# Score order by array half, and first-pass products of two heads issued in turn, in a macaron attention kernel

## What is computed

```python
        q = (qkv @ Wq + bq).reshape(B, S, H, dh).transpose(0, 2, 1, 3)
        k = (qkv @ Wk + bk).reshape(B, S, KVH, dh).transpose(0, 2, 1, 3)
        ...
        scores = jnp.einsum('bhgqd,bhkd->bhgqk', qg, k) * scale
        ...
        bias = slopes.reshape(KVH, G, 1, 1) * rel
        causal = jnp.tril(jnp.ones((S, S), dtype=bool))
        bias = jnp.where(causal, bias, -jnp.inf)
        attn = jax.nn.softmax(scores + bias[None], axis=-1)
        out = jnp.einsum('bhgqk,bhkd->bhgqd', attn, v)
```

## Time and profile before

| | |
|---|---|
| median of 3 runs | 739.92 us (739.89 to 741.77) |
| profiled execution, its own time | 740.43 us |
| its span on the core | 738.6 us |
| TensorE busy | 702.6 us (95%) |
| VectorE busy | 582.3 us (79%) |
| ScalarE busy | 403.3 us (55%) |
| reductions at L903, VectorE | 352 of them, 223.0 us, 681 ns each |
| L896, VectorE: reductions that also add the causal mask | 256 records, 149.3 us |
| attention, in the trace | from about 190 to about 600 us |

### The profile page before, as it was taken

How to read it: one execution, slowest core, us unless ns; L and a number is a source line. 1 busy time by engine, 2 the same in 40 slices (tenths; PEclk the granted TensorE clock), 3 DMA queues, 4 the chain that set the end, 5 groups by cost and what they waited for, 6 DMA issues and landing times.

```text
span 738.6 us, 15927 instructions
## 1 busy us (share of the span) xinstructions
PE 702.6 (95%) x5906; PEld 365.6 (50%) x5906; DVE 582.3 (79%) x1921; ACT 403.3 (55%) x579; POOL 112.6 (15%) x122
## 2 busy tenths in 40 slices
PE   8999998967999999999999999999999889999998
PEld 4554487833344444444444444444444255554598
DVE  6976468697999999999999999999999238766311
ACT  3353332132667777776777777677777743353300
POOL 3202882110000000000000000000000002103950
PEclk9999999975899999999999999999999999999999
DMA  8014533442010011001100100110010000005531
GB/s 217 1 16 77 93 64 113 144 139 85 25 38 26 27 26 40 20 21 38 33 26 20 39 20 22 39 38 20 21 39 1 2 1 0 2 1 91 107 92 58
DMA packets 47249, 34.69 MB, mean 47 GB/s; under 512 B 13106, under 2 KB 46514, under 8 KB 47172
## 3 DMA queue, kind: packets, MB, share of 16 engines
q1 hardware_dynamic: 46596, 33.60, 18.6%
q10 hardware_dynamic: 576, 0.08, 0.1%
HBM read 23.01 MB, written 10.39 MB: 45 GB/s over the span
## 4 chain that ended last, share of the span: by engine, by line
PE 52%; DVE 13%; issue 11%; ACT 2%; DVEq 0%; ACTq 0%
PE ps L1018 49%; DVE mx L903 8%; PE ps L1023 4%; DVE mx L896 1%; ACT h_all L624 1%; DVE h_all L896 1%; DVE xn L705 1%; DVE stats L693 0%; DVE wb L923 0%; DVE mm_ L920 0%; DVE sg L838 0%; ACT osb L613 0%; DVE idle L894 0%; DVEq L133 0%; DVE mv L697 0%
## 5 line engine op out<-in xcount | busy, mean ns | idle before, releaser
L624 ACT ACTIVATE h_all<-ps 128x1024 f32<-128x1024 f32 (+3 forms) x384 | 291.3, 810 | 112.4 <-PE ps L1018 109.2
L903 DVE TENSOR_REDUCE mx<-ps 128x1 f32<-128x512 f32 (+2 forms) x352 | 223.0, 681 | 9.2 <-PE ps L1018 5.8
L1018 PE MATMUL ps<-ks,xnT_all 57*128 57x512 bf16 (+3 forms) x768 | 178.9, 337 | 15.6 <-DVE mx L896 6.4
L1018 PE MATMUL ps<-h_all,vb 128*32 128x512 f32 (+3 forms) x1536 | 163.8, 500 | 0.6 <-ACT osb L613 0.6
L1018 PE MATMUL ps<-xnT_all,ks 59*128 59x512 bf16 (+3 forms) x768 | 158.6, 331 | 3.6 <-ACT h_all L624 3.4
L896 DVE CUSTOM_DVE_ANT_0 h_all<-ps,mask_w 128x384 bf16<-128x384 f32 (+1 forms) x256 | 149.3, 618 | 2.3 <-issue 0.7
L1018 PEld LDWEIGHTS ps<-ks,xnT_all 57*128 57x128 bf16 x768 | 56.5, 94 | 143.4 <-DVE mx L896 64.9
L1018 PE MATMUL ps<-cb 64*128 64x64 bf16 (+3 forms) x1216 | 113.0, 215 | 0.0
L717 DVE TENSOR_TENSOR h_all<-ps,sg 128x512 f32<-128x512 f32 x80 | 55.2, 690 | 50.5 <-PE ps L1018 48.8
L563 ACT ACTIVATE sg<-ps 128x512 f32<-128x512 f32 x80 | 47.8, 597 | 82.6 <-PE ps L1018 82.3
L1018 PEld LDWEIGHTS ps<-cb 64*128 64x128 bf16 x1216 | 80.1, 96 | 17.3 <-issue 0.7
(11 more groups left out here) (120 smaller groups left out, 553.6 us busy)
## 6 DMA issues: line engine op xcount, KB each, us to landing
xnT_all<-q_scr SPq DMA_DIRECT2D x64, 96.0 KB
attn<-sel_scr SPq DMA_DIRECT2D x12, 256.0 KB, 7.2
mask_second<-sel_scr SPq DMA_DIRECT2D x12, 256.0 KB, 8.2
q_scr<-qp SPq DMA_DIRECT2D x8, 384.0 KB
ks<-k_scr SPq DMA_DIRECT2D x64, 48.0 KB
x<-in_x SPq DMA_DIRECT2D x8, 256.0 KB, 5.7
yT<-sel_scr SPq DMA_DIRECT2D x8, 256.0 KB, 9.0
q_scr<-qp SPq DMA_DIRECT2D x8, 256.0 KB
```

The costliest lines, as they stand in the source:

```text
L624: act.activation(pr[:, (NSTEP * i + s) % PR_BUFS, p:HPG:SLOTS, lo:HALF], ps[:, b:b + 2, lo:HALF], ACT.Exp)\
L903: dve.tensor_reduce(m, src, AX.X, V.max).then_inc(a_out, 1)
L1018: return pe.matmul(o, l, r, start=start, stop=stop, skip_group_check=True)
```

## The change

Three things are changed.

- `score` issues the product of the half that the last piece did not use first, and its mask products in that order too. `RowsUsed.last` keeps the half of the last piece (0 upper, 1 lower) while the order is written out. Before, it was upper, then lower.
- Two merged pieces of the same shape that stand in the same group are issued by `two_pieces`: both banks are asked for first, then the products are issued one from each in turn, and each of the two last products raises `a_in`. This meets pieces 0 and 1 (step 0), 10 and 11 (step 3), 16 and 17 (step 5) of units 1 to 15, and 0 and 1 of unit 0.
- In `PER_STEP`, step 5 goes from (0, 2, 0, 1) to (0, 1, 0, 2): piece 16 moves from ahead of the step's second score pair to behind the product with V, where piece 17 already stood.

```diff
-PER_STEP = [(2, 1, 0, 0), (0, 1, 1, 0), (0, 2, 2, 1), (0, 2, 0, 0), (0, 3, 0, 0), (0, 2, 0, 1),
+PER_STEP = [(2, 1, 0, 0), (0, 1, 1, 0), (0, 2, 2, 1), (0, 2, 0, 0), (0, 3, 0, 0), (0, 1, 0, 2),
...
+            class RowsUsed:
+                last = 1
+
+            def piece_products(i, n, b):
...
+                RowsUsed.last = h0 // SLOTS
...
+            def two_pieces(i, n):
+
+                upper, lower = slot(a_out, NP1 * i + n + 1), slot(a_out, NP1 * i + n + 2)
+                for first, second in zip(piece_products(i, n, upper), piece_products(i, n + 1, lower)):
+                    pass
+                first.then_inc(a_in, 1)
+                second.then_inc(a_in, 1)
+                RowsUsed.last = PIECES[n + 1][1] // SLOTS
+
+            def pieces_of(i, some):
+
+                n = some.start
+                while n < some.stop:
+                    together = n + 1 < some.stop and PIECES[n][2] > 1 and PIECES[n][2:] == PIECES[n + 1][2:]
+                    if together:
+                        two_pieces(i, n)
+                    else:
+                        piece(i, n)
+                    n += 2 if together else 1
...
-                for r in range(2):
+                order = (1 - RowsUsed.last, RowsUsed.last)
+                for r in order:
                     at = RG * r
...
-                        for r in range(2):
+                        for r in order:
```

## The result

| | before | after |
|---|---|---|
| median, 6 runs each | 739.9 us (737.95 to 741.77) | 744.23 us (743.71 to 745.41) |
| ratio, 95% interval | | 1.0058 [1.0041, 1.0075] |
| span of the profiled execution | 738.6 us | 741.9 us |

The forecast was 743.0 us, in a range of 739.0 to 745.2, slower likeliest. It is slower, by 4.3 us where 3.1 were forecast. So the sign and most of the size were right, and 1.2 us are missing from the sum.

A forecast was written before the change was run, and what follows sets the result against it. The prediction took a TensorE chain that enters VectorE once per 25.70 us unit, at piece 17's reduction, as the bound. Terms 0 + 0 + 0 + 0.20 us over 15 units add 3.1 to 739.92: 743.0 us, range 739.0 to 745.2.

The forecast's parts named there:

- The bound: TensorE's chain per 25.70 us unit enters VectorE once, at piece 17's 0.70 us reduction (432.57); making it later lengthens the unit.
- Part 1: Turned score pairs, 12 of 24 a unit: lower product already overtakes the upper, so 0; at best 0.05 us.
- The first rival: Score products start in program order, so turned pairs in step 8 save up to 0.44 us a unit: 736.3 us; chance 0.16.
- Part 2: Pieces 0 and 1 issued in turn: they already run side by side, so 0.
- Part 3: Pieces 10 and 11 in turn: piece 10's reduction 0.25 us later, TensorE loses nothing; 0, at most 0.1 us a unit.
- the margin of 0.01 us at piece 14: Piece 11's reduction now ends at 428.71; with 0.05 for release, piece 14's start near 428.76 is met by 0.01 us.
- Part 4: Pieces 16 and 17 behind the product with V: TensorE 0.41 us ahead, piece 17's reduction late, 0.20 us a unit lost.
- Nothing is given back behind 434: From 434 to 440.7 the chain is TensorE's own work, so everything keeps its spacing and the 0.20 us delay stays.
- the rival "no change": VectorE's waits elsewhere, such as 0.28 us before 438.70, take up the delay: about 740 us; chance 0.17.
- The sum: All four parts, 0 + 0 + 0 + 0.20 us a unit over 15 units: 3.1 us slower, 743.0 us.

The follow-up runs named there:

- move_only: Kernel before with only step 5 of PER_STEP at (0, 1, 0, 2), piece 16 behind the product with V: 743.32 us, ratio 1.0043, unit +0.19 us.
- between: Kernel before with step 5 at (0, 1, 1, 1), piece 16 between the second score pair and the product with V: 738.15 us, ratio 0.9974, unit -0.10 us.
- flip_only: Kernel before with only the turned score pairs, the half not used last going first: 739.59 us, ratio 0.9994, unit 25.70 us.
- flip_wrong: Kernel before with each score pair starting with the half that was used last: 739.92 us, ratio 0.9996, unit 25.71 us.
- merge_load_apart: Kernel before with pieces 0/1 and 10/11 in turn, covered first-bank wait left out, load wait moved from piece 10 to 7: 740.88 us, ratio 1.0005, unit +0.09.
- merge_only: Kernel before with only pieces 0 and 1, and 10 and 11, issued in turn: 741.91 us, ratio 1.0023, unit +0.16 us.
- changed_load_apart: Whole changed kernel with the covered first-bank wait left out and the load wait moved from piece 10 to piece 7: 743.73 us, ratio 1.0054, unit +0.20.

## Why the prediction was right, and where it was not

- **The bound.** Right. The reduction at 432.57 sets the unit: in move_only, between and the changed kernel the unit moved by what that reduction moved, to 0.02 us, and the same operation in VectorE's slack cost nothing.
- **Part 1, score pairs, 0.** Right in both directions, flip_only and flip_wrong. The changed kernel's own step 8 looks like the earlier trace rows:

```profile
440.57 0.39 PE L1018 MATMUL ps<-ks,xnT_all 57*128 57x512 bf16 x1
440.58 0.33 PE L1018 MATMUL ps<-xnT_all,ks 59*128 59x384 bf16 x1
...
440.80 0.32 PE L1018 MATMUL ps<-xnT_all,ks 59*128 59x384 bf16 x1
```

  The first rival, faster by program order of the starts, falls with these and with the pair of step 5 above. It also speaks against the rule of the Trainium skill that the prediction weighed (TensorE: Matmul & The Clock Gate, The mechanism), that matmuls start strictly in program order: by it flip_wrong would have cost what flip_only gained, and neither did anything.
- **Part 2, pieces 0 and 1, 0.** Right as far as it can be seen: merge_load_apart's loss is accounted for by pieces 10 and 11. It wasn't run alone.
- **Part 3, pieces 10 and 11, 0 with a bound of 0.1.** The step that failed is the sentence that TensorE loses nothing because both pieces now do what piece 11 did. They do it 0.09 us later. I had the row of the double wait in hand (`[waits a_out,a_ld_second_even]` ahead of piece 10) and took the start of piece 11, which has a single wait, as its price. Everything behind followed: piece 10's reduction 0.34 late and not 0.25, piece 12's 0.17 and not 0.08. The stated bound of 0.1 a unit, 1.5 us, covered it by luck, since it was set for another reason, the margin of 0.01 us at piece 14. That margin did not decide: piece 14 starts 0.22 behind piece 12 before and after. The bank that VectorE's lateness reaches in merge_only is piece 16's, two pieces later, which I hadn't followed. With the late start taken away, the rest of part 3 holds in the changed kernel: changed_load_apart has piece 12 0.09 late and yet a unit of +0.20, the move alone.
- **Part 4, the move, 0.20 a unit.** Right, step by step. Product with V 0.53 behind piece 15; pieces 16 and 17 directly behind it and side by side; piece 17's reduction 0.61 behind piece 16's; piece 21 0.05 behind piece 18's end. Piece 16's reduction stands 0.83 behind piece 15's (434.27 - 433.44), not 0.9, because piece 15's was 0.16 late and TensorE, which delivers piece 16, only 0.10. move_only has it without that: 0.90, and a unit of +0.19.
- **Nothing is given back behind 434.** Right. From piece 18's reduction to VectorE's next wait the spacing is 5.39 us before and after (435.61 to 441.00):

```profile
441.00 2.73 DVE L903 TENSOR_REDUCE mx<-ps 128x1 f32<-128x512 f32 x4 [0.28 <-PE ps L1018]
```

  The wait of 0.28 is the same as in the earlier trace rows, so the rival "no change" falls too.
- **The sum.** Forecast 15 x 0.20 = 3.1 us, measured 4.3 in the medians and 4.2 by the unit. The mis-sized term is part 3's, put at 0: without its late start the unit falls from 25.98 to 25.91, unrounded by 0.08, and 15 x 0.08 = 1.2 us is what lies between 743.0 and 744.23.

## What to carry to other kernels

Before interleaving the two halves of the array by hand, look whether their products already start side by side; if so, the order pays nothing, and what counts is when the last product behind a semaphore is delivered to the engine that the chain of waits enters, and which instruction waits for that bank one turn of the ring later. A piece moved behind a longer product gives TensorE a lead that it can only spend waiting, if the reductions are the link: move it just so far that the reducing engine's queue has no gap (here 0.10 us a unit, and 0.20 lost by going one product further). When a wait is moved to an earlier instruction, see which waits that instruction already has.

## What the runs showed of the hardware that I had not expected

- **A second wait ahead of a first product costs 0.09 us.** With one wait, which the weight load carries, the product starts 0.046 us behind the release. With another semaphore's wait beside it, long satisfied, the late wait stands in a semaphore instruction of its own, and the product starts 0.135 us behind. What went with the 0.09 is that instruction: from three waits to two it stayed and nothing changed, from two to one it went. Two waits on the same semaphore alone were not run. Where the bank was long free, as at piece 10 before, the second wait is hidden.
- **The halves of the array are independent enough to make the written order void.** Two merged pieces of two products and two masks each run side by side when written one behind the other (move_only: four products in 0.40 us), and turning 13 of the 24 pairs, or the other 11, gives 0.9994 and 0.9996.
- **A delay of VectorE can travel unseen.** In merge_load_apart TensorE's own timing through pieces 10 to 15 is that of before to 0.02 us, while VectorE runs 0.1 us late; TensorE pays it at piece 16, six pieces behind the cause.
